# First attention: when VectorE adds a chunk into x, and where three seams stand in their queues

## What is computed

```python
xn = _layernorm(x)
s = _L0_attn_ref(xn, ...)            # gated linear attention, 16 heads of 16
g = _silu(_L0_ffn_ref(xn, ...))      # 8 experts, the best two of each token
x = x + s * g
xn = _layernorm(x)
s = _L1_attn_ref(xn, ...)            # softmax over a window of 64 tokens
g = _silu(_L1_ffn_ref(xn, ...))      # ternary weights, h = relu(...)^2
x = x + s * g
```

## Time and profile before

| | |
|---|---|
| time, median of 3 runs | 3459.67 us (3458.09 to 3459.83) |
| the profiled execution | 3460.7 us, of which the span is 3459.0 us |
| granted TensorE clock | 0.997 |
| busy share: TensorE, VectorE, ScalarE, GpSimd | 97%, 75%, 54%, 37% |
| matmuls in the profile | 34556 |

### The profile page before, as it was taken

How to read it: one execution, slowest core, us unless ns; L and a number is a source line. 1 busy time by engine, 2 the same in 40 slices (tenths; PEclk the granted TensorE clock), 3 DMA queues, 4 the chain that set the end, 5 groups by cost and what they waited for, 6 DMA issues and landing times.

```text
span 3459.0 us, 88576 instructions
## 1 busy us (share of the span) xinstructions
PE 3342.5 (97%) x34556; PEld 2274.0 (66%) x34556; DVE 2607.4 (75%) x6329; ACT 1863.8 (54%) x4135; POOL 1273.4 (37%) x1393
## 2 busy tenths in 40 slices
PE   6999999999999999999999999999999999999998
PEld 3676666766666666666666666666676666766666
DVE  6777867778677777877778777786777867778777
ACT  3364654646546465463655636456364653646546
POOL 4424244242442524325233342423434244242442
PEclk8999999999999999999999999999999999999999
DMA  4001010010110101011010100101001010010110
GB/s 105 18 22 47 24 38 19 24 44 24 38 23 24 40 24 47 14 38 26 24 50 11 50 18 20 49 12 49 18 23 45 24 38 23 20 44 24 38 23 26
DMA packets 98479, 109.59 MB, mean 32 GB/s; under 512 B 21153, under 2 KB 75025, under 8 KB 98065
## 3 DMA queue, kind: packets, MB, share of 16 engines
q1 hardware_dynamic: 93200, 102.25, 11.3%
q10 hardware_dynamic: 4864, 1.69, 0.2%
HBM read 74.01 MB, written 17.30 MB: 26 GB/s over the span
## 4 chain that ended last, share of the span: by engine, by line
PE 75%; DVE 12%; ACT 5%; issue 5%; POOL 1%; DMA 0%; DVEq 0%; SPq 0%; ACTq 0%; POOLq 0%
PE bank L1549 6%; PE bank L1508 5%; PE bank L1879 5%; PE bank L1647 5%; PE bank L1529 5%; PE bank L1781 5%; PE bank L1897 4%; PE bank L1719 4%; PE bank L1664 3%; PE bank L1619 3%; PE bank L1816 3%; PE bank L1842 3%; PE bank L1604 3%; PE bank L1713 2%; DVE am L1245 2%
## 5 line engine op out<-in xcount | busy, mean ns | idle before, releaser
L867 POOL TENSOR_TENSOR qx<-qx 128x512 f32<-128x512 f32 x256 | 277.3, 1088 | 658.7 <-ACT qx L1113 657.8
L1470 DVE TENSOR_TENSOR sq_lo<-qx,sq_hi 128x512 fp32r<-128x512 f32 x256 | 224.1, 875 | 177.1 <-ACT sq_hi L1092 176.6
L1378 DVE TENSOR_REDUCE row_max<-bank 128x4 f32<-128x384 f32 x512 | 270.8, 550 | 95.4 <-PE bank L1781 95.0
L1245 DVE TENSOR_TENSOR am<-bank,causal 128x512 f32<-128x512 f32 x512 | 328.1, 683 | 11.3 <-PE bank L1619 11.3
L988 ACT ACTIVATE tanh_g<-bank 128x256 f32<-128x256 f32 x128 | 49.3, 385 | 394.9 <-PE bank L1508 394.9
L1508 PE MATMUL bank<-w_vg,xt 128*128 128x512 f32 x512 | 252.3, 615 | 0.0
L1549 PE MATMUL bank<-xt,w_down 128*128 128x512 f32 x512 | 237.2, 596 | 0.0
L1897 PE MATMUL bank<-sq_hi,pj_t 128*128 128x512 f32 x512 | 213.2, 416 | 14.8 <-DVE sq_lo L1470 10.3
L1387 DVE TENSOR_TENSOR am<-bank,row_max 128x384 f32<-128x384 f32 x384 | 212.8, 554 | 9.8
L1113 ACT ACTIVATE qx<-bank,scale_fc 128x512 f32<-128x512 f32 x256 | 177.9, 695 | 70.9 <-PE bank L1884 69.0
L1032 ACT ACTIVATE am<-am 128x384 f32<-128x384 f32 x384 | 202.9, 528 | 8.5 <-DVE am L1387 8.5
(11 more groups left out here) (264 smaller groups left out, 8671.4 us busy)
## 6 DMA issues: line engine op xcount, KB each, us to landing
g_wide<-gate_rows SPq DMA_DIRECT2D x64, 512.0 KB, 6.0
x<-in_L_attn_x SPq DMA_DIRECT2D x128, 128.0 KB, 2.3
qt<-in_L_attn_x SPq DMA_DIRECT2D x128, 128.0 KB, 2.6
out<-x SPq DMA_DIRECT2D x128, 128.0 KB, 1.7
k<-k SPq DMA_DIRECT2D x96, 128.0 KB, 2.4
qt<-in_L_attn_x ACTq DMA_DIRECT2D x8, 128.0 KB, 7.6
x<-in_L_ffn_w_fc SPq DMA_DIRECT2D x1, 1024.0 KB, 5.9
attn<-in_L_ffn_w_proj SPq DMA_DIRECT2D x1, 1024.0 KB, 8.7
```

The source lines that it names most:

```text
L867: nc.gpsimd.tensor_tensor(sq[:, n % 3, :], relu[:, n % 3, :], relu[:, n % 3, :], ALU.mult)\
L1245: nc.vector.tensor_tensor(am_tiles[:, :, j], bank[3 + j][:].rearrange("p (f e t) -> p f e t", f=2, e=2), causal[:].unsqueeze(1).unsqueeze( ...
L1378: nc.vector.tensor_reduce(row_max[:, j, :], bank[1 + j][:, 0:4 * KW].rearrange("p (h k) -> p h k", k=KW), AX.X, ALU.max, negate=(j == 0)). ...
L1470: nc.vector.tensor_tensor(sq_lo[:, n % 3, :], sq[:, n % 3, :], sq_hi[:, n % 3, :].bitcast(F32), ALU.subtract)\
```

## The change

There are five edits, on four engines.

1. VectorE: `finish_chunk` of chunks 0 to 3 moves from the end of the following chunk's round to the middle of the round after that, between `f_gates` and `state_sum`. Chunk 4's stays at the end of round 5, chunk 5's and later stay where they were. GpSimd's `rstd2(0, 0, 4)`, which needs the four `veps`, moves from the middle of round 5 to its end.
2. ScalarE: a one-column Exp on `gdiff` (`warm`, its result is not read) stands between `experts_relu(2)` and `experts_relu(3)`. It waits for no semaphore.
3. VectorE: in rounds 1 and 2 of the second attention `attention_bias` stands ahead of the last `maxima` and `shifted` instead of behind them.
4. GpSimd: `head_rstd` stands behind the squares of steps 5 and 8 instead of 4 and 7.
5. VectorE: `head_normalise` pairs stand in steps 6, 7, 9 and 10 instead of 6 to 9.

```diff
--- before.py
+++ after.py
@@ -111,6 +111,7 @@
     gdiff = sb("gdiff", [P, NC])
     gexp = sb("gexp", [P, NC])
     gden = sb("gden", [P, NC])
+    warm = sb("warm", [P, 1])
     g_top = sb("g_top", [P, 2, NC])
     g_hit = sb("g_hit", [P, 2, NC, E])
     g_all = sb("g_all", [P, NC, E])
@@ -293,6 +294,7 @@
              "nxn_ok hqp_ok hqk_ok").split()
     s = {n: sem(n) for n in names}
     out_parts = (bank[6][:, 0:D], bank[1][:, D:2 * D])
+    normalise_steps = (6, 7, 9, 10)
     turn_steps = (MT + 2, MT + 3, MT + 5, MT + 6)
     pair_turn_banks = (2, 1, 3)
     turn_banks = {6: 7, 7: 0}
@@ -828,8 +830,6 @@
                     for c in range(NC):
                         if c:
                             norm_affine(c - 1)
-                        if c == NC - 3:
-                            rstd2(0, 0, 4)
                         if c == NC - 1:
                             rstd2(1, 4, NC - 2)
                         if c + 1 < NC:
@@ -845,6 +845,8 @@
                                 pool.wait_ge(s["at_ok"], at("at_ok", 4 * c))
                             parity_queries(c + 1)
                             hidden_gated(c + 1)
+                            if c == NC - 3:
+                                rstd2(0, 0, 4)
 
                     norm_rstd(NC - 1)
                     rstd2(2, NC - 2, NC - 1)
@@ -866,8 +868,8 @@
                             pool.wait_ge(s["sql_ok"], at("sql_ok", n - 2))
                         nc.gpsimd.tensor_tensor(sq[:, n % 3, :], relu[:, n % 3, :], relu[:, n % 3, :], ALU.mult)\
                           .then_inc(s["sq_ok"], 1)
-                        if n in (4, 7):
-                            head_rstd(pool, n // 7)
+                        if n in (5, 8):
+                            head_rstd(pool, n // 8)
                 now["copy"] = 0
 
             @block.scalar
@@ -915,6 +917,7 @@
                         act.wait_ge(s["gtp_ok"], at("gtp_ok", b + 1))
                         nc.scalar.copy(gate_rows[:, b * 512:(b + 1) * 512], bank[gate_banks[b]][32:64, :]).then_inc(s["gx_ok"], 1)
                     experts_relu(2)
+                    nc.scalar.activation(warm[:], gdiff[:, 0:1], ACT.Exp)
                     experts_relu(3)
                     def decays(c):
 
@@ -1293,6 +1296,8 @@
                             gated_output(c - 1)
                         if c + 1 < NC:
                             experts_gate(c)
+                        if 2 <= c < NC - 2:
+                            finish_chunk(c - 2)
                         if c == NC - 2:
                             dve.wait_ge(s["rs2"], at("rs2", 1))
                             for b in range(4):
@@ -1326,7 +1331,7 @@
                         if c + 1 < NC:
                             if c:
                                 project_gated(c - 1)
-                            if 0 < c < NC - 2:
+                            if c == NC - 3:
                                 finish_chunk(c - 1)
                             middle_state(c + 1)
                             if c < NC - 2:
@@ -1427,9 +1432,11 @@
                         shifted(4 * c + 5)
                         maxima(4 * c + 6)
                         shifted(4 * c + 6)
+                        if 0 < c < 3:
+                            attention_bias(c - 1)
                         maxima(4 * c + 7)
                         shifted(4 * c + 7)
-                        if c:
+                        if c >= 3:
                             attention_bias(c - 1)
                         attention_out(c)
                         if c < 3:
@@ -1479,9 +1486,10 @@
                                 head_stats(dve, c)
                         if n == 3:
                             head_moments(dve)
-                        if 6 <= n < 10:
-                            head_normalise(dve, 2 * (n - 6))
-                            head_normalise(dve, 2 * (n - 6) + 1)
+                        if n in normalise_steps:
+                            p = normalise_steps.index(n)
+                            head_normalise(dve, 2 * p)
+                            head_normalise(dve, 2 * p + 1)
                         if n == NG * MT - 2:
                             head_low_split(dve, 1)
                     finish2(3)
```

## The result

The changed kernel takes 3424.02 us (median of 4 runs, 3420.17 to 3425.67), the one before 3459.56 in the same session: a ratio of 0.9897, 95% interval 0.9879 to 0.9914, 35.5 us faster. 3429 was forecast, with 3422 to 3440 as the range.

What follows compares the result with a forecast made beforehand. TensorE, busy 97%, was taken as the bound. Per sequence 0.82 - 0.20 + 0.35 - 0.05 + 0.70 - 0.10 + 0.44 = 1.96 us, times 16 about 31.5 off 3460.7: 3429 us, range 3422 to 3440.

Steps and rivals of the forecast that it cites:

- five starts of TensorE that were picked: Late starts at L1619, chunk 5's state product, L1756 (chunks 1 and 2), L1897: gains 0.82, 0.35, 0.70, 0.44 us a sequence.
- the charge for the gap: VectorE ahead of `state_sum`: the moved sum-into-x set overruns its idle time in round 5, charged 0.05 us a sequence.
- 2.01 against 1.94, an overrun of 0.07: Round 5, VectorE: the set needs 1.25 plus a 0.76 wait for GpSimd; room is 1.45 + 0.84 - 0.35.
- room of 2.27: Round 4, VectorE ahead of `state_sum`: idle gap of 1.43 plus 0.84 because VectorE arrives earlier.
- The give-back at L1647: At `experts_up`, TensorE, 0.82 ahead, waits for GpSimd's gated hidden tile behind the gates' DMA: 0.20 us a sequence lost.
- slack of 0.62: At `experts_up`, the gated hidden tile's 0.66 to spare in one sequence, less about 0.04 for a semaphore.
- The charge on edit 3: Second attention: later subtraction leaves VectorE about 0.06 of its 0.41 idle before the next maximum; charged 0.10 us a sequence.
- The rivals: One gain given back 0.12; table load holds longer 0.04; late rounds 0.05; slower 0.02; edits do nothing 0.02.
- drain: ScalarE table switch: the skill's 1380 ns after the 1283 ns load; by it the sum would be about 0.8 smaller.
- The rival of the late rounds: VectorE does not arrive earlier, so `state_sum` is 0.58 late in rounds 4 and 5: 3452 us, chance 0.05.

Runs made afterwards that it cites:

- the four single kernels: The kernel before with only edit 2, only edit 1, only edit 3, or edits 4 and 5 together: 3445.99, 3454.67, 3447.06 and 3450.77 us.
- the fully split kernel: Changed kernel with only the statistics of chunks 0 to 4 moved to the later round, their sums into x behind `sf`: 3405.85 us.

## Why the prediction was right

**Which waits go.** All five starts of TensorE that were picked lost their wait, and each was worth what the row said: 0.83 for 0.82, 0.35 for 0.35 in chunk 5, 0.71 for 0.70, 0.44 for 0.44. That they are independent is shown by the four single kernels, whose gains add up to the whole within the spread of the runs.

**The 0.10 behind a wait.** The working counted only the wait. The matmul after it is another 0.10 late in chunks 4 and 5 and in the feed-forward part, three times a sequence, 5 us in all. At the other two places, L1619 and L1756, it is not: behind L1756 the difference is under 0.01. In chunk 4 the wait itself was 0.015 and the matmul behind it still lost 0.105, which I read as nothing to gain. This and the small steps are more than the 4 us by which the sum fell short; the charge for the gap was short the other way. It was in the rows: L1897 is 0.50 long where it waited and 0.40 elsewhere.

**The charge for the gap, 0.05 against 0.31.** The step "2.01 against 1.94, an overrun of 0.07" had the right wait: 0.77 measured, 0.76 used. The room was wrong, and for the most part one round earlier. On time, `state_sum` starts 0.31 behind the start of TensorE's last matmul of the update (rounds 0 to 5 before the change, in the mean over the sequences). After it, this is 0.53 in round 4 and 0.63 in round 5: 0.21 and 0.31 late. For round 4 the working had a room of 2.27, enough for 2.01, with `o_norm` ahead of it 0.84 earlier. But the `o_norm` at the end of round 3 comes only 0.40 earlier, 4.80 behind its `state_sum` instead of 5.20. There GpSimd's multiplication waits for its input from ScalarE, and `o_rstd` stands behind it in GpSimd's queue:

```profile
1590.50 1.26 POOL L821 TENSOR_TENSOR attn<-attn,g_wide 128x512 f32<-128x512 f32 x1 [5.39 <-ACT attn L909]
1591.73 0.40 POOL L787 TENSOR_SCALAR o_veps<-o_mom 128x1 f32<-128x1 f32 x1
1592.21 0.57 POOL L791 TENSOR_TENSOR o_rstd<-o_veps,minus_half 128x1 f32<-128x1 f32 x1
...
1592.81 0.41 DVE L1216 TENSOR_SCALAR o_norm<-o_tok,o_mom,o_rstd 128x256 f32<-128x256 f32 x1 [0.77 <-POOL o_rstd L791]
```

TensorE's lead is also larger than the 0.35 that was taken off: 0.12 from chunk 4, and 0.45 in chunk 5 with the matmul behind. So 0.21 of the give-back was carried over from round 4, and round 5 itself added 0.10, near the 0.07 of the working. In the kernels above in which `x` does not wait for GpSimd ahead of it, `state_sum` is back at 0.31 in rounds 0 to 5.

**The give-back at L1647, 0.20 against 0.27.** Right in size by luck: one sequence's slack of 0.62 stood for sixteen that differ by over a microsecond. What TensorE lost there in the mean, with the matmul behind, was 0.11, 0.14, 0.15, 0.20, 0.22 and 0.32 in six traces in which the load was moved and the transfer left as it was. It may also be why the changed kernel's runs differ by 5.5 us; this was not tested run by run.

**The charge on edit 3, 0.10 against nothing.** VectorE's idle time ahead of the next maximum did shrink, from 0.41 to 0.27 in the mean and not to the 0.06 of the working, so it still takes up all of the shift.

**The rivals.** None came about as it was priced. No drain shows around the table load: 0.02 ahead of it and 1.29 from its start to the next activation's. The Trainium skill's figure of 2.66 us for a switch ("ScalarE: Activation LUTs", "What ACT_TABLE_LOAD costs") is not what this kernel pays, 1.28. The rival of the late rounds came nearest: `state_sum` is late in rounds 4 and 5, as it said, but by 0.21 and 0.10 more, not by 0.58 in each. With chunk 4's set in round 6 as well the kernel is 4.2 slower than the changed one, about as much as edit 1 alone had won (4.1).

## What to carry to other kernels

Before you move an instruction into an idle gap, look at what GpSimd runs there and whether a trace shows this kind of instruction held beside it. Here a sum of two tiles of 0.42 cost 1.19 in one gap and 0.42 in another, a normalisation of one tile took 1.04 instead of 0.40, and the statistics (0.43) took their own time in both. Count what a removed wait can also take from the matmul behind it, and let every gain of the bounding engine shrink the gap of the next round before you fit work into it. When you count on an engine to arrive earlier, look for the next thing that it waits for: `o_norm` was held by a value that stood behind other work in GpSimd's queue. A slack that ends in a DMA is read from all repetitions, not from one, and a transfer whose first quarter is wanted first can be sent in two.

## What the runs showed of the hardware that was not expected

- A matmul directly behind one that waited starts about 0.10 later at some places (0.105 in the state product, even where the wait was 0.015; 0.103 at L1897; 0.10 at L1655), and not at others (under 0.01 at L1764 and at the turns, L1635). What divides them was not tested.
- While GpSimd multiplied, VectorE's sum of two tiles in SBUF took 1.19 instead of 0.42, and a `tensor_scalar` of one tile was held up as well: 1.13 instead of 0.40 in `head_normalise` before the change, 1.04 instead of 0.40 in round 6. `bn_stats` was not: 0.41 to 0.43.
- A table load in a gap that is too short costs the overlap and nothing more: with 1.28 and an Exp of 0.20 ahead of it, the relu behind it was late, and TensorE lost nothing beyond one start of 0.09 that the next matmul made up.
- The gates' broadcast lands 4.7 to 7.4 us after its issue in one and the same program (median 6.1 of the fully split kernel).
